# Order of the opening of a fused cross-attention and FFT-FFN kernel: keys first, half the zero products

## The reference, cut to what matters

```
# x (2, 2048, 512), context (2, 128, 512), mask (2, 1, 2048, 128), 16 heads of 32
q = layernorm(x) @ wq + bq;  k = ctx @ wk + bk;  v = ctx @ wv + bv
score = (q . k) / sqrt(32) * mask
score = where(score == 0, -1e9, score)
x = x + softmax(score) @ v @ wo + bo
y = real(ifft(fft(layernorm(x)) @ (wr + i wi)))
x = x + y + bias
```

## Time and profile before

| | |
|---|---|
| median of 3 runs | 457.48 us (457.0 to 458.08) |
| profiled execution | 456.98 us |
| its span, first to last instruction | 455.2 us |
| TensorE busy | 433.3 us (95%) |
| VectorE busy | 403.5 us (89%) |
| ScalarE busy | 368.3 us (81%) |
| GpSimd busy | 353.0 us (78%) |

### The profile page before, as it was taken

The page is one execution under the profiler, slowest core; times in us unless marked ns, Lnnn a source line. Parts: engine busy times, 40 slices in busy tenths (PEclk is TensorE's granted clock), DMA queues, the critical chain, the costliest instruction groups (busy, mean ns, idle before and its releaser), DMA issues.

```text
span 455.2 us, 10923 instructions
## 1 busy us (share of the span) xinstructions
PE 433.3 (95%) x3510; PEld 298.5 (66%) x3510; DVE 403.5 (89%) x538; ACT 368.3 (81%) x1342; POOL 353.0 (78%) x476
## 2 busy tenths in 40 slices
PE   6989897998999999999999999999999999989997
PEld 5777676777566676666676666666766665555444
DVE  3797699889999999999999999999999899999353
ACT  3358597789998989998989899899989899999620
POOL 6588844685879989798989898989899877755763
PEclk9999999999999999999999999999999999999999
DMA  8996662332426455564555445546443424341244
GB/s 287 389 376 183 234 199 70 93 92 60 107 72 153 109 156 115 141 133 125 117 153 117 132 87 138 128 123 153 108 104 66 109 69 115 55 92 24 71 110 122
DMA packets 85287, 60.15 MB, mean 132 GB/s; under 512 B 40142, under 2 KB 72814, under 8 KB 84719
## 3 DMA queue, kind: packets, MB, share of 16 engines
q1 hardware_dynamic: 84508, 59.29, 48.4%
q10 hardware_dynamic: 722, 0.17, 0.2%
HBM read 29.33 MB, written 8.39 MB: 83 GB/s over the span
## 4 chain that ended last, share of the span: by engine, by line
PE 58%; DVE 14%; POOL 10%; issue 8%; ACT 7%; DMA 1%; ACTq 1%; POOLq 0%; DVEq 0%
PE bank L454 24%; PE bank L459 15%; PE bank L611 7%; ACT zs L714 5%; PE bank L625 4%; DVE zs L904 4%; PE scores L599 3%; DVE zs L897 3%; PE bank L560 2%; POOL cl L1146 2%; POOL rzb L1140 2%; POOL xs L1093 2%; ACT pt L723 1%; PE bank L541 1%; DMA bqb<-in_bq 1%
## 5 line engine op out<-in xcount | busy, mean ns | idle before, releaser
L714 ACT ACTIVATE zs<-zs,nbias 128x128 f32<-128x128 f32 x512 | 199.5, 395 | 18.1 <-POOL nbias L1133 17.3
L714 ACT ACTIVATION_READ_ACCUMULATOR zs<-zs,nbias 128x1 f32 x512 | 98.4, 192 | 0.0
L904 DVE SCALAR_TENSOR_TENSOR zs<-zs 128x1024 f32<-128x1024 f32 x64 | 89.7, 1401 | 1.2
L909 DVE TENSOR_REDUCE nmin<-zs 128x8 f32<-128x1024 f32 x64 | 78.1, 1220 | 2.2
L897 DVE TENSOR_TENSOR zs<-scores,ms 128x1024 f32<-128x1024 f32 x64 | 78.1, 1220 | 1.0 <-issue 0.6
L723 ACT COPY pt<-bank 128x512 f32<-128x512 f32 x128 | 67.8, 580 | 13.5 <-PE bank L611 13.4
L611 PE MATMUL bank<-ident,zs 128*128 128x128 f32 x512 | 66.8, 273 | 1.9 <-ACT zs L714 1.9
L459 PE MATMUL bank<-xth,wqh 128*128 128x256 f16 x224 | 61.2, 273 | 1.3 <-DVE ql L869 1.3
L1093 POOL TENSOR_TENSOR xs<-xs,bob 128x512 f32<-128x512 f32 (+1 forms) x41 | 42.9, 1049 | 25.0 <-DVE zs L904 21.9
L459 PE MATMUL bank<-xtl,wqh 128*128 128x256 f16 x224 | 61.1, 273 | 0.0
L459 PE MATMUL bank<-xth,wql 128*128 128x256 f16 x224 | 61.1, 273 | 0.0
(11 more groups left out here) (126 smaller groups left out, 929.2 us busy)
## 6 DMA issues: line engine op xcount, KB each, us to landing
xs<-in_x SPq DMA_DIRECT2D x16, 512.0 KB, 4.5
xtr<-in_xt SPq DMA_DIRECT2D x16, 512.0 KB, 4.5
out<-x SPq DMA_DIRECT2D x31, 256.0 KB, 2.5
qs<-qh SPq DMA_DIRECT2D x120, 64.0 KB
lp<-in_lparts SPq DMA_DIRECT2D x4, 1024.0 KB, 8.3
qs<-ql SPq DMA_DIRECT2D x60, 64.0 KB
ms<-in_mask SPq DMA_DIRECT2D x16, 128.0 KB, 2.6
wqs<-in_wq SPq DMA_DIRECT2D x2, 512.0 KB, 6.9
```

Of the source, the lines that this page charges most:

```text
L714: last = act.activation(z, z, ACT.Exp, bias=nbias[:, s % 4, i:i + 1], scale=-NEG, accum_out=zsum[:, s % 4, i:i + 1])
L904: dve.scalar_tensor_tensor(out=z, in0=z, scalar=0.0, in1=z, op0=ALU.is_equal, op1=ALU.subtract).then_inc(eq_done, 1)
L909: dve.tensor_reduce(nmin[:, s % 4, :], zs[:, s % NZ].rearrange("p t h k -> p (t h) k"), AX.X, ALU.min).then_inc(mn_done, 1)
```

## The change

The order of fills in the opening becomes CT, CT, K 0, K 1, W1 0, ST 0, Q ...: both key halves ahead of the column sums and of all query fills. The loads, ScalarE's, VectorE's and GpSimd's lists are put into an order that fits; among other things `moments(1)` moves from ahead of the first key half to behind ("Q", 0, 1), and GpSimd's `spread_k(1)` from behind four folds to ahead of `stat_cols(1)`. The 28 products of zeros become 14. No instruction of another kind is added or removed.

```diff
@@ -41,8 +41,8 @@
 
 
     fills, slots, held = [], {}, []
-    lead = [("W1", 0), ("CT", 0), ("CT", 1), ("K", 0), ("ST", 0), ("Q", 0, 0), ("Q", 0, 1), ("S", 0),
-            ("W1", 1), ("Q", 0, 2), ("S", 1), ("K", 1), ("Q", 0, 3), ("ST", 1), ("Q", 1, 0), ("S", 2),
+    lead = [("CT", 0), ("CT", 1), ("K", 0), ("K", 1), ("W1", 0), ("ST", 0), ("Q", 0, 0), ("Q", 0, 1), ("S", 0),
+            ("W1", 1), ("Q", 0, 2), ("S", 1), ("Q", 0, 3), ("ST", 1), ("Q", 1, 0), ("S", 2),
             ("Q", 1, 1), ("Q", 1, 2), ("Q", 1, 3)]
     front = []
     for f in lead:
@@ -386,16 +386,16 @@
                 n = slice(256 * i, 256 * i + 256)
                 sp.dma_start(dst[:, :, n], w_view(w)[:, :, n]).then_inc(done[i], 16)
 
-            load_half(wqs, wq, 0, d_wq)
-            load_x(0)
-            load_xt(0)
             sp.dma_start(ident[:], eye).then_inc(d_eye, 16)
             sp.dma_start(cxs[:], ctx_in.rearrange("b k d -> k b d")).then_inc(d_cx, 16)
             load_half(wks, wk, 0, d_wk)
+            load_x(0)
+            load_half(wks, wk, 1, d_wk)
+            load_half(wqs, wq, 0, d_wq)
+            load_xt(0)
+            load_half(wqs, wq, 1, d_wq)
             load_x(1)
             load_mask(0)
-            load_half(wqs, wq, 1, d_wq)
-            load_half(wks, wk, 1, d_wk)
             load_xt(1)
             load_parts(0)
             load_x(2)
@@ -631,7 +631,7 @@
                     pe.matmul(CX[:, 0:256], qh[:, 1, 0, 0:128], qh[:, 1, 1, :], start=True, stop=True)
 
             pe.wait_ge(p_zero, 3)
-            zeros(28)
+            zeros(14)
             for item in front + [i for v in range(V0, V1) for i in slots[v][0]]:
                 if item[0] == "S":
                     scores(*item[1:])
@@ -748,21 +748,21 @@
                 act.wait_ge(d_wq[i], 16)
                 act.activation(wqh[:, :, n], wqs[:, :, n], ACT.Identity, scale=SQ).then_inc(w_hi, 1)
 
+            act.wait_ge(d_eye, 16)
+            act.copy(ident16[:], ident[:]).then_inc(i16_done, 1)
+            hi(at["K", 0])
             high_q(0)
             split_hi(0)
-            act.wait_ge(d_eye, 16)
-            act.copy(ident16[:], ident[:]).then_inc(i16_done, 1)
+            hi(at["K", 1])
             hi(at["W1", 0])
-            hi(at["K", 0])
             hi(at["ST", 0])
+            hi(at["Q", 0, 0])
             high_q(1)
-            hi(at["Q", 0, 0])
             hi(at["Q", 0, 1])
             split_hi(1)
             hi(at["W1", 1])
             hi(at["Q", 0, 2])
             exps(0, 0)
-            hi(at["K", 1])
             exps(0, 1)
             hi(at["Q", 0, 3])
             hi(at["ST", 1])
@@ -989,30 +989,30 @@
                                          op0=ALU.mult, op1=ALU.subtract).then_inc(w_lo, 1)
 
             dve.memset(bqb[:], 0.0).then_inc(b_zero, 1)
-            low_q(0)
-            moments(0)
-            lo(at["W1", 0])
             lo(at["CT", 0])
             lo(at["CT", 1])
+            moments(0)
+            lo(at["K", 0])
+            low_q(0)
+            spread_k(0)
             split_lo0()
-            moments(1)
-            lo(at["K", 0])
-            spread_k(0)
+            lo(at["K", 1])
+            lo(at["W1", 0])
             lo(at["ST", 0])
             lo(at["Q", 0, 0])
+            low_q(1)
             lo(at["Q", 0, 1])
-            low_q(1)
+            moments(1)
             mask_mul(0)
             lo(at["W1", 1])
             zero_to_neg(0)
             least(0)
             lo(at["Q", 0, 2])
-            moments(2)
+            spread_k(1)
             mask_mul(1)
             zero_to_neg(1)
-            lo(at["K", 1])
-            spread_k(1)
             least(1)
+            moments(2)
             lo(at["Q", 0, 3])
             lo(at["ST", 1])
             moments(3)
@@ -1194,9 +1194,9 @@
             pool.wait_ge(p_zero, 3)
             pool.wait_ge(p_kz, 1)
             stat_cols(0)
+            spread_k(0)
             scale_mask(0)
-            pool.wait_ge(p_ms, 1)
-            spread_k(0)
+            spread_k(1)
             stat_cols(1)
             split_lo(1)
             fold(0)
```

## The result

The changed kernel takes 462.29 us (median of 4 runs, 460.85 to 464.09) against 457.24 us of the kernel before beside it (4 runs, 456.97 to 458.08): a ratio of 1.0114, with a 95% interval of 1.0097 to 1.0132. Slower was the forecast, but by 1.2 us, and it is 5.0. The profiled execution took 461.28 us with a span of 459.5, which is 4.3 us more on either count, so 4.3 us is what its trace can explain. Repeated later, the same kernel gave 461.96 us (5 runs, 461.12 to 462.94; ratio 1.0102, 1.0088 to 1.0115).

What follows compares the result with a forecast made beforehand. Bound: start of TensorE's unbroken run at ("Q", 1, 1), set by VectorE's subtraction. VectorE's sum was 1.0 us late, GpSimd's chain 1.5; taking 1.2, 457.48 + 1.2 = 458.7 us, range 456.0 to 460.8.

Steps and rivals of the forecast that it cites:

- the lower bound of that term: GpSimd from stat_cols(1) to bias(0): 8.6 us taken, 7.6 with both folds at their lower end.
- The late `moments(1)`: VectorE's moments(1) ends at 24.05, delaying GpSimd's stat_cols(1), bias(0) and ScalarE's exponentials; that chain ends 1.5 us late.
- I count that as taken up: ScalarE and VectorE lag more after ("Q", 1, 1), but their spare 1.8 and 1.5 us from 40 to 50 absorb it.
- spread_k(1) (1.3): VectorE's four small copies after 22.2 us, counted at 1.3 us in its sum of work.
- the sum for VectorE: Work without a gap from 22.2 us, 13.8 us, ending the subtraction of ("Q", 0, 3) at 36.3, 1.0 us late.
- the port rule: GpSimd and VectorE lock one shared port pair per instruction; split_lo(1) would wait 0.8 us, folds run free, end 1.3 late.
- the chain through GpSimd: bias(0) near 32.65, eight exponentials to 36.0, copy of ("Q", 0, 3) behind them, VectorE's low part at 36.75: 1.5 late.
- slow keys: Rival: TensorE's clock is low during the key fills, the first takes 7.4 us instead of 3.7; 462.4 us, chance 0.04.
- The 14 left out cost nothing, since TensorE idled behind them: At TensorE's start, dropping 14 of the 28 products of zeros was costed at nothing.
- up to 1.7: At the context transposes in the new order, leaving out the 14 zero products is worth up to 1.7 us.

Runs made afterwards that it cites:

- kernel 4: Changed kernel with VectorE's moments(1) moved up into its idle time behind ST 0: 460.34 us, ratio 1.0075.
- kernels 1 to 6 and 10: Of these, 1 is the changed kernel with VectorE's spread_k(1) earlier: 462.45 us; 2 has ScalarE's (Q, 0, 3) and ST 1 copies ahead of the exponentials: 462.92.
- kernel 7: Changed kernel with 44 products of zeros in TensorE's wait inside ("Q", 1, 0): 461.51 us, ratio 1.0099.
- kernel 8: Kernel before with 14 products of zeros at the start instead of 28, nothing else: 459.17 us, ratio 1.0056.
- kernel 6: Changed kernel with 28 products of zeros at the start again: 463.39 us, ratio 1.0140.
- kernel 3: Changed kernel with spread_k(1) earlier on VectorE and ScalarE's copies of (Q, 0, 3) and ST 1 ahead of the first exponentials: 458.96 us, ratio 1.0044.
- kernel 9: Kernel 3 with 18 products of the identity ahead of ("Q", 1, 1): 458.44 us, ratio 1.0028.
- kernel 10: Kernel 5 with 20 identity products ahead of ("Q", 1, 1) and GpSimd's folds 2 and 3 moved behind split_lo(2): 457.59 us, ratio 1.0010.
- kernel 11: Kernel before with GpSimd's folds 2 and 3 moved behind split_lo(2), nothing else: 458.68 us, ratio 1.0025.
- kernel 5: Kernel 3 with VectorE's moments(1) also moved up behind ST 0: 458.63 us, ratio 1.0045.

## Why the forecast had the sign and not the size

**What held.** TensorE's first key fill, both fills back to back, ("Q", 0, 0), `low_q(1)` (20.89, forecast 21.0), the end of `moments(1)` (23.86; 24.05) and `stat_cols(1)` (24.02; 24.05) are within 0.35 us. The context landed at 5.3 (4.8), without harm. `bias(0)` is 0.8 early, since the two folds ran at 1.25 us each: the lower bound of that term. The late `moments(1)` is a cost as described; kernel 4 puts 2.0 us on it. The shift at the first value fill, 4.03, is at the end 4.3; in kernels 1 to 6 and 10 the two also agree within 0.3 us. In 7, 8 and 9 the end adds 0.9 to 1.4, by waits of TensorE that the kernel before doesn't have: 0.86 us for `qs` at 87.38 in kernel 7, 0.95 and 0.48 us for VectorE's mask product at 63.30 and 60.37 in 8 and 9. In 11 it adds 2.5. So "I count that as taken up" held for the changed kernel, and not where TensorE began early and VectorE didn't.

**The step that failed first** is the term "spread_k(1) (1.3)" in the sum for VectorE: 1.3 was the duration of copies with little beside them, and the new place puts them beside `split_lo(1)` and two folds. They measured 3.82. The excess of 2.5 us is the whole difference between the end of the subtraction in the forecast (36.3) and in the trace (38.59), 2.3; the two `zero_to_neg` (1.22 and 2.15 for 1.6 each) almost cancel. The forecast used the port rule for the folds' sake only and asked what they lose, not who loses to them.

**The second** is the sentence on the chain through GpSimd that names only "the copy of ("Q", 0, 3)" behind the eight exponentials. The next entry of the list, `hi(at["ST", 1])`, is what ("Q", 1, 0) needs for its last product, and S 2 is behind that. By the forecast's own times this copy ends at about 36.6, S 2 runs from 37.0 to 38.3, and ("Q", 1, 1) starts there instead of at 36.5: that is 3.0 us late, and 460.5 in place of 458.7. In the kernel before the exponentials came early enough for this wait not to exist.

**The third** follows from the second: a pause of 4.94 us took the clock with it, which the sum doesn't have; filling it gave 0.8 us, within the noise of the two kernels (kernel 7). The rival "slow keys" looked for a slow clock at the keys, where it wasn't (7.14 us for both); what varied ahead of them is the pace of the transposes.

**A reason that was wrong without harm** is "The 14 left out cost nothing, since TensorE idled behind them". In the kernel before leaving them out costs 2.2 us (kernel 8), 1.4 of them seen in the trace as the slower pace of what comes after. In the changed kernel the context lands as they end, and leaving them out is worth 1.1 to 1.4 us (kernel 6), within the "up to 1.7" of the forecast, with more scatter.

Of the 5.0 us, the two gates together are 3.3 (kernel 3 against the changed one), the pause that is left 0.5 when it is filled, and `moments(1)`'s chain with the folds beside `zero_to_neg` 0.9 (from kernel 9 to 10); some 0.4 is left, and the interval of kernel 10 just excludes no change. The 3.3 are clear of noise and explained; the 0.5 isn't clear of noise, and the 0.9, whose intervals just touch, belongs to three edits at once. These shares depend on the order in which they are taken: `moments(1)` alone gives 2.0, and nothing once the gates are gone.

## What to carry to other kernels

A duration read at one place belongs to its neighbours too: before moving a small copy, look at what GpSimd does at the new place, not at the old one. When an engine's start moves, go down its list past the first entry that somebody waits for, and for each entry name the last product that needs it. Two gates within 0.2 us of each other make every single undo look like a miss, so try them in pairs before dropping either, and look in each trace whether the one edit moved the other gate, as the first did here.

## What the runs showed of the hardware that was not expected

- How hard one GpSimd instruction hits small copies on VectorE: a copy of 32 x 256 f16 elements, 0.22 to 0.43 us in the kernel before, took up to 1.19 us, until the GpSimd instruction beside it had ended. GpSimd's small ones are hit alike: `bias` 1.21 us instead of 0.26 in kernel 11.
- A pause of TensorE can cost behind it as well. After 4.94 us idle the granted clock was 0.50 for 6.8 us, about three of them idle and the other four work at half pace. But the length of the pause alone doesn't tell: in kernel 3 the clock fell after one of 2.27 us, in kernel 5 it stayed at 1.00 through one of 3.24.
- The pace of the first microseconds differs between executions of the same start: 28 products took 4.80, 5.21 and 5.97 us (the kernel before, kernels 11 and 6), all with a granted clock of 1.00 on the page.
